# Layer 0: fifteen gathers of slot rows issued one at a time, each after the landing of the one before

## The chip, the cores and the metric

The kernel runs on one core of a Trainium2 chip, written instruction by instruction for five engines (TensorE, VectorE, ScalarE, GpSimd, SyncE) that meet only at semaphores. The metric is the device time of one execution in microseconds, median of several timed executions. A separate execution, taken by the hardware profiler, gives the page and the trace.

## What is computed

Two layers, each a conditioning step and a mixture of experts, on 1024 tokens (32 x 32) of width 256. Layer 0 is where the change is:

```
x1 = x + ffn0(cond0(x)),   x2 = x1 + ffn1(cond1(x1))

cond0:  out[b] = x[b] @ w[subject[b]]                      # one of 8 matrices of 32 x 32 for each b
ffn0:   gate = softmax(xf @ Wr.T)                          # 8 experts
        top-2 experts of each token; rank of the token in its expert; kept if rank <= 320
        y[n] = sum over kept e of gate[n, e] * ((silu(xf @ Wg[e].T) * (xf @ Wu[e].T)) @ Wd[e].T)
```

The capacity of an expert is 320 tokens; an expert's inner width is 176. Layer 1 (a gated unit of width 1024 with adapters, then 16 experts with top 4 and a shared expert) starts from x1, all of it.

## The kernel before

Layer 0 computes two of the eight experts densely for all tokens, and six only for the tokens that chose them. For the six, token rows are brought into slots: 320 slots for each expert, two experts share 640 slots, which are five tiles of 128 (PAIR_TILES); the middle tile of a pair (SHARED_AT = 2) holds 64 slots of each expert. So there are fifteen slot tiles, i = 0 to 14, numbered along the three pairs of experts. The experts are q = 0 to 5.

The stage runs like this:

- All 1024 rows of the conditioned input lie in DRAM (`x2`, written by SyncE). VectorE computes `get`, the token of each slot (L1109, semaphore `q_get`), and `put`, the row of the scatter.
- GpSimd gathers: `gather0(i)` (L603 to L607) issues one indirect DMA of 128 rows of 1 KB, into one of twelve buffers `q_xg`. It counts on `q_in[q]`, 16 for each gather; q is the first expert that needs the tile, so tiles 0, 1, 2 count for expert 0, tiles 3, 4 for expert 1, and so on for each pair. The order of the calls is written out by hand (L615 to L629): five gathers at once, then each further one behind a wait for TensorE (on `q_turn`, an expert's rows transposed, or on `q_gu`, three for each expert, its gate and up products), because it reuses a buffer or to spread the traffic.
- TensorE, for each expert in order: `q_turn_in(q)` waits for `q_in[q]` and transposes the rows (L1573); ScalarE and VectorE split them in two parts (L789 to L793, L1135 to L1139); `q_gate_up(q)` forms the products (L1500 to L1502); ScalarE takes the silu and VectorE the product; `q_down(q)` (L1605, L1606) projects back, with the next expert's transposes and gate products between. ScalarE copies the result out (`q_rows`, L807), VectorE the shared tile (L1156).
- GpSimd scatters: `scatter0` (L609 to L611, shown in the profile as L610) writes each of the fifteen tiles to its rows of `y_k` in DRAM. All scatters stand behind all gathers in GpSimd's program (L632 to L639).
- SyncE waits for all fifteen scatters (L531, L532), loads the rows back (L534), GpSimd, ScalarE and VectorE weigh and add the two choices of each token (L648, L811, L1198), TensorE adds them (L1620) to what the dense experts gave, and VectorE forms x1 (L1205).

The weights of each sparse expert are loaded by SyncE (L503, L510), each waiting for a buffer. TensorE fills the time behind the last sparse expert with products of the dense experts.

Of the kernel before, what the change touches and what calls it, by code (L numbers as in the profile page):

```python
# [31 lines left out]
PAIR_TILES = PAIR_SLOTS // P  # L32
SHARED_AT = CAP // P
# [84 lines left out]
def build(nc, d):  # L118
    with ExitStack() as ctx:
# [264 lines left out]
        q_in, q_st, q_rw, q_dw = t_in[0:ES], s_y[0:ES // 2], s_w1[0:2], s_w1[2:5]  # L384
# [200 lines left out]
        def _(pool):  # L585
# [14 lines left out]
                                  ).then_inc(s_ct, 1)  # L600
            nc.gpsimd.tensor_copy(planes[:].rearrange("p k t -> p (k t)"), cst1[:, CT_TOK:CT_TOK + NT * K1]).then_inc(s_ct, 1)

            def gather0(i):  # L603
                j = i % Q_XG
                q = i // PAIR_TILES * 2 + (i % PAIR_TILES > SHARED_AT)
                nc.gpsimd.indirect_dma_start(q_xg[j], None, d["x2"], bass.IndirectOffsetOnAxis(ap=get[:, i:i + 1], axis=0)
                                             ).then_inc(q_in[q], 16)  # L607

# [6 lines left out]
            for i in range(PAIR_TILES):  # L615
                gather0(i)
            pool.wait_ge(q_turn, 1)
            gather0(PAIR_TILES)
            for n in range(3):
                pool.wait_ge(q_gu, n + 1)  # L620
                gather0(PAIR_TILES + 1 + n)
# [83 lines left out]
        def _(act):  # L705
# [124 lines left out]
            for q in range(ES):  # L830
# [9 lines left out]
                if 2 <= q < 4:  # L840
                    hid_high(L0, q - 2, q - 2)
            _, hi, _ = w_of(ED)
            act.wait_ge(s_raw[0], 32)
            act.wait_ge(q_gu, 3 * (ES - 1))
# [650 lines left out]
        def _(pe):  # L1495
# [356 lines left out]
            def tile_gate_up(i, e):  # L1852
                par, ps = i % 2, tile_gu(i)
                pe.wait_ge(t_xh, i + 1)
                if i == 1:
                    pe.wait_ge(s_silu, 2 * (c + NA))
                elif i == 2:
                    pe.wait_ge(s_prod, 2 * (c + NA))
                elif i > 2:
                    pe.wait_ge(t_hd, i - 1)  # L1860
                whole = [[w[:, bass.ds(e * GU_N, GU_N)] for w in pair_of] for pair_of in ((w1_hi, w1_lo), (w1_hi1, w1_lo1))]
                k_part = [slice(k * P, (k + 1) * P) for k in range(KH)]
                for k, (w_hi, w_lo) in enumerate(whole):
                    T.matmul(ps, xgT_hi[par][:, k_part[k]], w_hi, start=k == 0, stop=False)  # L1864
                    T.matmul(ps, xgT_hi[par][:, k_part[k]], w_lo, start=False, stop=False)  # L1865
                pe.wait_ge(t_xl, i + 1)
                for k, (w_hi, _) in enumerate(whole):
                    last = T.matmul(ps, xgT_lo[par][:, k_part[k]], w_hi, start=False, stop=k == KH - 1)  # L1868
                last.then_inc(t_gu, 1)
# [205 lines left out]
```

## Time and profile before

| | us |
|---|---|
| timed runs, median of 3 | 393.48 |
| lowest and highest | 391.77, 394.31 |
| span of the profiled execution | 424.4 |
| TensorE busy in it | 382.7 |
| GpSimd busy in it | 188.6 |
| mean granted TensorE clock (1.0 is 2.4 GHz) | 0.968 |

The profiled execution is one of its own, 31 us longer than the median of the timed ones; its times are read against its own span. An instruction at GpSimd that issues a DMA is shown for the time of its issue; when the data lands is seen in the chain of waits, or where the DMA engines go idle. The label of a tile is the name of the buffer underneath it: the gathered rows appear as w_hi_f, expert weights as w_hi_f or w_raw, the rows of the scatter as w_dn or sg_b, and the conditioned input as x.

### The profile page before, as it was taken

What the parts mean: (1) busy time and instruction counts of PE and PEld (TensorE: products, weight loads), DVE (VectorE), ACT (ScalarE), POOL (GpSimd) and SP (SyncE); (2) the same over time, 40 slices, a digit from 0 to 9 for tenths busy, and PEclk for the clock granted to TensorE, in tenths of its full rate; (3) what the DMA queues carried; (4) which work ended last, traced back from release to release, by engine and by line L of the source; (5) the groups of instructions that cost most, each with busy time, mean ns of one, the idle gap of its engine ahead of it and who ended that gap; (6) DMA issues with size and microseconds to landing.
All of it is one profiled execution on the core that took longest, in us unless ns stands there. A gap on an engine that the chain in (4) does not pass through costs nothing.

```text
span 424.4 us, 6202 instructions
## 1 busy us (share of the span) xinstructions
PE 382.7 (90%) x1984; PEld 328.6 (77%) x1984; DVE 221.2 (52%) x533; ACT 147.6 (35%) x304; POOL 188.6 (44%) x176
## 2 busy tenths in 40 slices
PE   3998869999999999999999996788987779999996
PEld 3877869787888888888777885687876668899885
DVE  6894554289512211221779763734454324656557
ACT  2644265244534433342554252412122111322140
POOL 0625653563255454423212277355665566444600
PEclk9999989999999999999989999898988898999999
DMA  6965353275233333111013785222222233111285
GB/s 213 386 253 165 101 175 113 74 260 192 88 114 124 125 124 124 39 38 37 2 37 101 181 195 169 62 73 70 85 88 74 72 90 85 61 57 64 77 317 190
DMA packets 22004, 51.89 MB, mean 122 GB/s; under 512 B 3878, under 2 KB 9510, under 8 KB 21670
## 3 DMA queue, kind: packets, MB, share of 16 engines
q1 hardware_dynamic: 16022, 35.24, 25.0%
q0 software_dynamic: 5952, 16.26, 12.6%
q8 instruction: 18, 0.29, 0.3%
q14 instruction: 12, 0.10, 0.1%
HBM read 38.12 MB, written 13.37 MB: 121 GB/s over the span
## 4 chain that ended last, share of the span: by engine, by line
PE 63%; DVE 11%; another core or an unknown queue 9%; DMA 5%; issue 5%; POOL 3%; ACT 2%; SPq 1%; POOLq 0%; DVEq 0%; ACTq 0%
PE gu L1500 9%; PE gu L1501 9%; PE gu L1502 9%; PE y L1889 7%; PE gu L1864 4%; PE gu L1868 3%; PE gu L1865 3%; PE y L1500 2%; PE y L1501 2%; PE y L1502 2%; PE gu L1526 2%; DMA w_raw<-y_k 1%; PE gu L1813 1%; PE gu L1791 1%
## 5 line engine op out<-in xcount | busy, mean ns | idle before, releaser
L591 POOL TENSOR_TENSOR w_lo<-w_raw,w_hi 128x768 fp32r<-128x768 f32 (+3 forms) x26 | 34.4, 1344 | 76.8 <-ACT w_hi L716 60.4
L681 POOL DMA_INDIRECT y_k<-w_raw,put x47 | 46.2, 984 | 49.9 <-DVE w_raw L1417 41.5
L1500 PE MATMUL gu<-act_hi,w_hi 128*128 128x512 f32 x132 | 53.6, 406 | 0.8 <-DVE hid L1023 0.8
L1501 PE MATMUL gu<-act_lo,w_hi 128*128 128x512 f32 x132 | 52.4, 397 | 0.0
L1864 PE MATMUL gu<-w_hi,xgT 128*128 x94 | 40.3, 429 | 12.1 <-ACT xgT L899 8.7
L1023 DVE TENSOR_TENSOR hid<-silu,gu 128x512 f32<-128x512 f32 x24 | 16.5, 687 | 66.6 <-PE gu L1502 66.5
L1502 PE MATMUL gu<-act_hi,w_lo 128*128 128x512 f32 x124 | 48.9, 394 | 0.0
L944 ACT ACTIVATE silu<-gu 128x176 f32<-128x176 f32 x47 | 14.9, 317 | 90.7 <-PE gu L1868 55.8
L1410 DVE TENSOR_TENSOR hid<-silu,gu 128x176 f32<-128x176 f32 x47 | 15.7, 334 | 48.8 <-ACT silu L944 30.6
L1865 PE MATMUL gu<-w_lo,xgT 128*128 x94 | 32.2, 343 | 0.0
L745 ACT ACTIVATE hid_hi<-hid 128x512 fp32r<-128x512 f32 x24 | 15.2, 631 | 47.3 <-DVE hid L1023 47.3
L1864 PEld LDWEIGHTS gu<-w_hi,xgT 128*128 128x128 f32 x94 | 18.9, 201 | 15.5 <-issue 14.3
L1500 PEld LDWEIGHTS gu<-act_hi,w_hi 128*128 128x128 f32 x132 | 25.1, 190 | 6.3 <-DVE hid L1023 1.2
L1501 PEld LDWEIGHTS gu<-act_lo,w_hi 128*128 128x128 f32 x132 | 25.2, 191 | 5.2
L1500 PE MATMUL gu<-lora_store,w_hi 128*128 128x512 f32 (+2 forms) x68 | 25.2, 370 | 4.5 <-DVE lora_store L1135 4.1
L732 ACT ACTIVATE silu<-gu 128x512 f32<-128x512 f32 x30 | 17.7, 595 | 29.8 <-PE gu L1502 29.0
L1502 PEld LDWEIGHTS gu<-act_hi,w_lo 128*128 128x128 f32 x124 | 23.7, 191 | 5.3
L1889 PE MATMUL y<-w_dn,t_hidT 88*128 x96 | 26.6, 404 | 0.0
L1417 DVE COPY w_raw<-y 128x256 f32<-128x256 f32 x47 | 19.7, 418 | 10.5 <-remote 5.2
L1868 PE MATMUL gu<-w_hi,xgT 128*128 x94 | 24.5, 344 | 0.0
L1501 PE MATMUL gu<-lora_store,w_hi 128*128 128x512 f32 (+2 forms) x68 | 24.3, 357 | 0.0
L1889 PE MATMUL y<-w_dn,silu 88*128 x92 | 23.8, 380 | 0.0
(325 smaller groups left out, 905.3 us busy)
## 6 DMA issues: line engine op xcount, KB each, us to landing
w_raw<-in_w_gu SPq DMA_DIRECT2D x16, 352.0 KB, 4.6
w_raw<-in_wc SPq DMA_DIRECT2D x8, 576.0 KB, 5.0
w_raw<-y_k SPq DMA_DIRECT2D x5, 512.0 KB, 5.7
w_hi_f<-in_w0s SPq DMA_DIRECT2D x6, 368.0 KB
y_k<-hid SPq DMA_DIRECT2D x1, 2048.0 KB, 13.3
w_dn<-in_w_dn SPq DMA_DIRECT2D x1, 1936.0 KB
w_raw<-in_ws SPq DMA_DIRECT2D x5, 384.0 KB, 3.0
w_hi_f<-y_k SPq DMA_DIRECT2D x6, 256.0 KB, 4.4
```

The lines of the kernel that those rows point to most:

```text
L591: nc.gpsimd.tensor_tensor(w_lo[par][:, w], w_raw[par][:, w], w_hi[par][:, w].bitcast(F32), ALU.subtract).then_inc(split, 1)
L681: nc.gpsimd.indirect_dma_start(d["y_k"], bass.IndirectOffsetOnAxis(ap=put[:, i:i + 1], axis=0), t_out[j], None).then_inc(s_y[j], 16)
L732: A.activation(silu[s][rows(tail)], gate, ACT.Silu).then_inc(s_silu, 1)
L1023: V.tensor_tensor(out[rows(tail)], silu[s][rows(tail)], up[rows(tail)], ALU.mult).then_inc(s_prod, 1)
L1417: V.tensor_copy(t_out[j], out_ps[i % 2]).then_inc(t_put, 1)
L1500: T.matmul(out, w[0], x[0], start=start, stop=False)
L1501: T.matmul(out, w[0], x[1], start=False, stop=False)
L1502: return T.matmul(out, w[1], x[0], start=False, stop=stop)
L1864: T.matmul(ps, xgT_hi[par][:, k_part[k]], w_hi, start=k == 0, stop=False)
L1865: T.matmul(ps, xgT_hi[par][:, k_part[k]], w_lo, start=False, stop=False)
L1868: last = T.matmul(ps, xgT_lo[par][:, k_part[k]], w_hi, start=False, stop=k == KH - 1)
L1889: last = T.matmul(out_ps[i % 2], t_hidT[i % DEPTH][:, k], w1_dn[0:HALF_I, bass.ds((e * 2 + k) * H, H)], start=k == 0, stop=k == 1)
```

## The change

Ahead of each gather but the first, GpSimd waits until the gather before it has landed: for the count of `q_in` that the previous tile belongs to, at 16 for every gather of that count so far. The function that gives a tile its count gets a name, `pair_of`. The waits for TensorE between the gathers stay, as do their order, buffers and sizes. Scatters and layer 1 are as before.

```diff
+            def pair_of(i):
+                return i // PAIR_TILES * 2 + (i % PAIR_TILES > SHARED_AT)
+
             def gather0(i):
                 j = i % Q_XG
-                q = i // PAIR_TILES * 2 + (i % PAIR_TILES > SHARED_AT)
+                q = pair_of(i)
+                if i:
+                    pool.wait_ge(q_in[pair_of(i - 1)], 16 * sum(pair_of(n) == pair_of(i - 1) for n in range(i)))
                 nc.gpsimd.indirect_dma_start(q_xg[j], None, d["x2"], bass.IndirectOffsetOnAxis(ap=get[:, i:i + 1], axis=0)
                                              ).then_inc(q_in[q], 16)
```

## Rows read from the trace of the kernel before

**Rows 1.** The page: its head and the busy time of each engine.

```profile
span 424.4 us, 6202 instructions
...
PE 382.7 (90%) x1984; PEld 328.6 (77%) x1984; DVE 221.2 (52%) x533; ACT 147.6 (35%) x304; POOL 188.6 (44%) x176
```

**Rows 2.** Timeline, GpSimd: start, duration (us), line, op, out<-in [idle before, releaser].

```profile
29.04 1.14 POOL L606 DMA_INDIRECT w_hi_f<-x,get  x1 [10.04 <-DVE get L1109]
...
37.16 0.94 POOL L606 DMA_INDIRECT w_hi_f<-x,get  x1 [1.93 <-PE y L1573]
...
50.84 0.95 POOL L606 DMA_INDIRECT w_hi_f<-x,get  x1 [0.30 <-issue]
...
54.73 1.00 POOL L610 DMA_INDIRECT y_k<-w_dn,put  x1 [2.95 <-ACT w_dn L807]
...
68.04 0.97 POOL L610 DMA_INDIRECT y_k<-w_dn,put  x1 [4.12 <-ACT w_dn L807]
...
84.10 0.97 POOL L610 DMA_INDIRECT y_k<-w_dn,put  x1 [0.30 <-issue]
```

**Rows 3.** Chain of waits, 28 to 60 us: start, duration (us), what.

```profile
31.75 3.65 DMA w_hi_f<-x,get
...
36.01 0.87 PE y L1573 x6
...
48.55 4.75 another core or an unknown queue
```

**Rows 4.** Timeline, TensorE (L1573 is transposes, L1500 and L1606 products).

```profile
39.08 0.38 PE L1500 MATMUL gu<-lora_store,w_hi 128*128 128x320 f32 x1 [0.41 <-issue]
...
41.79 0.60 PE L1573 MATMUL y<-cst,w_hi_f 128*128 128x128 f32 x4
...
46.57 0.81 PE L1573 MATMUL y<-cst,w_hi_f 128*128 128x128 f32 x6
...
49.38 0.59 PE L1606 MATMUL y<-w_hi_f,w_dn 128*128 128x256 f32 x2
...
59.47 0.38 PE L1500 MATMUL gu<-lora_store,w_hi 128*128 128x320 f32 x1 [2.58 <-DVE lora_store L1135]
...
63.73 0.82 PE L1573 MATMUL y<-cst,w_hi_f 128*128 128x128 f32 x6
...
69.61 0.60 PE L1573 MATMUL y<-cst,w_hi_f 128*128 128x128 f32 x4
...
95.30 1.39 PE L1620 MATMUL y<-cst,w_hi_f 128*128 128x128 f32 x11
```

**Rows 5.** Chain of waits, 80 to 100 us.

```profile
84.10 2.42 DMA y_k<-w_dn,put
...
86.53 0.03 SPq L532
...
98.52 0.68 DVE xT L1205
```

**Rows 6.** Windows: length, busy per engine, TensorE's clock, DMA share, GB/s.

```profile
34.00:36.00 2.00, 0.84 (x8) 0.65 (x6) 1.05 (x2) 1.18 (x2) 0.95 (x1) 1.00 0.99 303
...
39.50:40.50 1.00, 1.00 (x9) 1.00 (x8) 0.00 (x0) 0.27 (x1) 0.04 (x1) 1.00 0.00 0
...
57.00:59.40 2.40, 0.00 (x0) 0.00 (x0) 2.34 (x6) 2.35 (x4) 0.38 (x1) 1.00 0.60 148
...
60.00:62.00 2.00, 2.00 (x9) 2.00 (x9) 1.13 (x2) 0.44 (x1) 1.70 (x2) 0.50 0.27 105
...
86.25:86.50 0.25, 0.25 (x2) 0.20 (x2) 0.22 (x1) 0.25 (x1) 0.25 (x1) 1.00 0.00 0
```

**Rows 7.** Timelines of ScalarE and SyncE, as in rows 2.

```profile
53.32 0.60 ACT L807 ACTIVATE w_dn<-y 128x512 f32<-128x512 f32 x1 [4.77 <-remote]
...
53.31 0.33 SPq L510 DMA_DIRECT2D w_hi_f<-in_w0s  x1
...
81.66 0.60 ACT L807 ACTIVATE w_dn<-y 128x512 f32<-128x512 f32 x1 [2.19 <-PE y L1606]
```

## Prediction

> **What bounds the kernel now.** I read the page's head first: TensorE is busy for 382.7 of 424.4 us, so the kernel as a whole hangs on TensorE and on what it waits for [rows 1]. The change touches one stage, from 29 to 98 us of the profiled execution, so the answer lies in three chains of that stage: the gathers, TensorE, and the scatters behind the gathers.
>
> The timeline of GpSimd shows fifteen gathers at L606, first and last start 29.04 and 50.84 us. An issue takes 0.95 us (the first 1.14) and the next starts 0.30 us later, so a back-to-back gather costs GpSimd 1.25 us; at 37.16 us it waited for TensorE instead [rows 2]. Then come fifteen scatters at L610, from 54.73 to 85.07 us, 0.97 us each plus 0.30 us. They are not back to back: the one at 68.04 us waited 4.12 us for ScalarE's copy L807. So GpSimd has slack in this stage, between 52 and 68 us above all.
>
> TensorE waits for a landing only once: the chain of waits has the third gather as a transfer from 31.75 us for 3.65 us, and after an issue gap the first transposes at 36.01 us [rows 3]. The later groups of transposes (start 41.79, 46.57, 63.73 and 69.61 us for experts 1, 2, 4 and 5; expert 3's are like them) come straight behind a product of TensorE, with no idle time before them [rows 4]. The end of the stage is double. The last scatter is issued at 84.10 us and landed 2.42 us later; only then does SyncE (L532) load the scattered rows back, and the chain of waits runs through this reload to the layer-1 input at 98.52 us [rows 5]. TensorE's own products of the stage last until 95.30 us, where it begins to add the reloaded rows, again without idle time before it [rows 4]. So either chain, if it is later, delays everything after it; the later of the two decides. Layer 1 begins with that input, so what is lost here is lost at the end.
>
> **What one gather costs when the next waits for it.** No row shows this wait, so I bound it. The gather at 37.16 us runs alone: the DMA engines are idle from 39.50 us on [rows 2, 6]. Its data has moved 2.34 us after its issue began. The completion comes after the last packet: of the last scatter, packets end by 86.25 us and the wait ends at 86.52 us, 0.3 us later [rows 5, 6]. So a lone gather lands in 2.34 + 0.3 = 2.64 us. GpSimd's reaction to a semaphore is read at 37.16 us: the transposes it waited for end at 36.88 us, so 0.28 us [rows 2, 3]. Period: 2.9 us in place of 1.25. Lower bound: the scatter's 2.42 us, the same kind of transfer, + 0.28 = 2.7 us [rows 5]. Upper bound: the third gather, beside three weight loads and its two forerunners, took 36.01 - 31.75 = 4.26 us, so 4.5 us with the reaction [rows 3]. I take 2.9, since the DMA engines are free between gathers once those loads are in (share 0.00 from 39.5 to 40.5 us [rows 6]), and 4.26 us for the second gather alone, which is issued at 32.2 us beside those weight loads (DMA share 0.99 from 34 to 36 us [rows 6]). The weight loads that follow later (one pair for each expert, the first at 53.31 us [rows 7]) will meet a gather three or four times; I add 1.5 us for all, and 0 and 6 us are the ends of that.
>
> The Trainium skill has a price of its own (page "DMA: Bandwidth & Descriptors", section on the anatomy of one DMA from GpSimd): about 2.0 us fixed plus the bytes over 436 GB/s, for 128 KB 2.3 us. With the reaction that would be a period of 2.6 us, and by the sums below no loss at all. The row, 2.64 us for the landing, does not agree with it, and I go by the row.
>
> **Step by step.** Gather 0 at 29.04 us. Gather 1 at 29.04 + 0.19 + 2.64 + 0.28 = 32.2 us, landed at 36.4. Gather 2 at 36.7, landed 39.4: the first transposes start at 39.4 instead of 36.0 us. Gathers 3 and 4 land at 42.3 and 45.2; TensorE comes to their transposes 5.8 us after the first ones (41.79 - 36.01 [rows 3, 4]), at 45.2: no further wait. Gathers 5 to 7 are issued at 45.5, 48.4, 51.3 and land by 53.9: expert 2's transposes start at 53.9 instead of 46.6, +7.3 us. Gathers 8, 9 land at 59.7, when TensorE comes to expert 3. Before, the products of expert 3 started only at 59.47 us, after a wait of 2.58 us for VectorE [rows 4]: a chain of ScalarE and VectorE work leads to them that starts with the copy at 53.32 us [rows 7] and takes 6.15 us. It needs expert 0's down products, which ended 3.4 us after expert 2's transposes began (49.97 - 46.57 [rows 4]), so it starts at 57.3 and the products at 63.5 us; at either clock (2.7 or 4.3 us, below) they are over by 67.8 us. Gathers 10 to 12 land at 68.4 against 63.73 (+4.7), 13 and 14 at 74.2 against 69.61 (+4.6). With the 1.5 us of contention the last is issued at 73.1 us and lands at 75.7 (+6.1). GpSimd's older waits for TensorE (on transposes and gate products) are passed long before at each of these times, so they add nothing. From expert 5's transposes to ScalarE's last copy it was 81.66 + 0.60 - 69.61 = 12.65 us [rows 4, 7]: 88.3 us.
>
> **What is queued behind the waiting gathers** is every scatter: none can be issued before gather 14 has been (73.1 + 0.95 us). Scatter 1 then starts at 74.35 instead of 54.73 us, and fifteen at 1.27 us run back to back until 74.35 + 14 x 1.27 + 0.97 = 93.1 us. Are they ready? The last three need the copy at 88.3 us and their turn comes at 89.6 us: yes. Before, the last ended at 85.07 us. So GpSimd's chain is **+8.0 us**, TensorE's only +6.1 us, and the former decides. Behind the scatters, in GpSimd's queue, stand two splits (L642, 3 us, hidden by the reload) and the weighting L648; SyncE's reload of the rows, then its loads of layer-1 weights, wait for the same landing and move with it. I price these at the same +8.0 us, not more, for they keep their order.
>
> TensorE's clock: it idled from 57.0 to 59.4 us and ran at half its speed (granted 0.50, the 1.2 GHz level) at 60 to 62 us; the products from 59.47 to 63.73 us took 4.3 us, those from 39.08 to 41.79 us 2.7 us [rows 4, 6]. After the change TensorE waits 4 us twice (35 to 39, 50 to 54 us) and 2 us before expert 4. Each may cost 1.6 us on TensorE; the first two are covered by the next landing, the third by the 1.3 us between 88.3 and 89.6 us but for 0.3 us. I put 0; without cover it is 1.6 us each.
>
> **The hold.** ScalarE's copy at 53.32 us and SyncE's load at 53.31 us both waited for a product that TensorE had finished by 50.0 us; the chain books 4.75 us on an unknown party [rows 3, 4, 7]. That held up ScalarE, then VectorE, and led to the 2.58 us wait and the half clock. The profiled span of 424.4 us is 31 us above the 393.48 us median of the timed runs, so something in it is not in them. If this hold isn't, the stage before is shorter by the 3.3 us from 50.0 to 53.3 and by the 1.6 us of the half clock (4.3 - 2.7), which comes from the idle time that it leads to: 4.9 us. After the change the gathers set the pace and nothing is gained: the loss would be 8.0 + 4.9 = 12.9 us. I take half of it, 2.4 us. Sum: 393.5 + 8.0 + 2.4 = **403.9 us** (in terms of the profile 424.4 + 8.0 = 432.4 us).
>
> **Rivals.**
> (a) Not slower: a landing costs the 2.42 us of the scatter and nothing contends. Period 2.7, gather 14 at 66.8 us, first scatter at 68.1, last ended at 68.1 + 18.8 = 86.8 us: +1.7 us, 395.2 us. The point from which it decides is a period of 2.57 us, where 29.04 + 14 p + 1.25 + 18.8 is 85.07 us: below it GpSimd's slack between 52 and 68 us swallows everything. By the Trainium skill's price above the kernel would be there, at 393.5 us. Against it: the lone gather's 2.34 us before any completion. If the hold is only in the profile, the point is 2.22 us. Chance 0.11.
> (b) All gathers are as slow as the third was: period 4.5, last scatter 29.04 + 63 + 1.25 + 18.8 = 112.1 us: +27 us, 420.5 us. For it: the gathers share the engines with weight loads. Against: from 39.5 to 40.5 us the engines are idle [rows 6], and the next weight load is issued at 53.31 us [rows 7]. Chance 0.03; a milder form, three or four gathers at 4.3 us (+6 in place of +1.5 us) gives 408.4 us, chance 0.15.
> (c) Faster, since gathers in flight at once were in one another's way: the third took 4.26 us. Its landing would have to come before 36.0 us with two forerunners awaited, and it is issued only at 36.7 us. I see no mechanism; chance 0.02.
> (d) The change does nothing, the waits being met already: excluded for most, as back-to-back issues are 1.25 us apart and a landing takes over 2.4 us; this is included in (a).
> (e) My sum, with the hold in the timed runs (401.5 us) or not (406.4 us): chance 0.69.
>
> **How the numbers follow.** (e) alone spans 400 to 407. The range takes the milder (b) and reaches towards (a): 397.5 to 410 us leaves out most of (a), the strong (b) and (c). About 1%, 3.9 us, is what a measurement of this kernel can tell from no change. Slower by over 1% (above 397.4 us): (b) and (e), 0.87. Within 1%: (a), 0.11. Faster: (c), 0.02.
>
> **What would show it.** In the profile after: starts at L606 about 2.9 us apart (2.6 or less: (a); over 3.5: (b)); first transposes at about 39.4 us; expert 2's at 54 us with a wait of some 4 us on a landing; the last gather at about 73 us; fifteen scatters 1.27 us apart with hardly a wait on L807 between; the last ending near 93 us. I am wrong if the scatters still wait for ScalarE, or if TensorE's products after expert 5 end later than the scatters.

## The result

| | kernel before | changed kernel |
|---|---|---|
| timed, median (us) | 391.77 | 414.8 |
| lowest and highest | 391.32 to 394.31 | 412.5 to 415.5 |
| ratio, 95% interval | | 1.0555 (1.0515 to 1.0595) |
| span of the profiled execution | 424.4 | 410.7 |

The change costs 23.0 us by the medians and 5.6% by the ratio, which is 21.8 us. The forecast had the direction and the order of events right and less than half of the size (10.4 of 23.0 us): 403.9 us, with 410 as the upper end. Medians and ratios here and below leave out executions that lie over 1.5% above the fastest of the same kernel timed beside them, among them one of 475 us and two of 949 us.

The two spans contradict the times: the changed kernel's is the shorter one. The experiments below show that the kernel before takes 425 to 429 us on one chip and 392 to 395 us on three others. The trace that the prediction was made from is like the trace from the first (span 424.4 beside 426.8 us, the same hold), so it is taken to come from a chip of that kind; which chip it was isn't on record. So the readings below set the trace of after beside a second trace of the kernel before, from a chip of the quick kind (run e8_before_again, 392.14 us). Its page, head and busy times:

```profile
span 390.1 us, 6202 instructions
...
PE 369.3 (95%) x1984; PEld 319.4 (82%) x1984; DVE 220.5 (57%) x533; ACT 147.2 (38%) x304; POOL 189.3 (49%) x176
```

and that of the changed kernel, with TensorE's busy share and its granted clock in 40 slices:

```profile
span 410.7 us, 6211 instructions
...
PE 372.6 (91%) x1984; PEld 321.6 (78%) x1984; DVE 221.3 (54%) x533; ACT 147.3 (36%) x304; POOL 190.2 (46%) x176
...
PE   3994848499989999999999999998999999999995
...
PEclk9999989699999999999999999999999999999999
```

Of the 20.6 us by which the span is longer, TensorE is busy for 3.3 us more (372.6 against 369.3 us) and waits for the other 17.3 us. The dents of TensorE's line lie in slices 4 to 8 (31 to 82 us), and the mean clock falls in the same stretch (to 8 and 6 tenths in slices 6 and 8). The rest of the line is nearly as before.

The timeline of GpSimd in the kernel before (e8_before_again), first and last gather, first and last scatter; columns as in [rows 2]:

```profile
29.24 1.14 POOL L606 DMA_INDIRECT w_hi_f<-x,get  x1 [10.27 <-DVE get L1109]
...
50.87 0.95 POOL L606 DMA_INDIRECT w_hi_f<-x,get  x1 [0.30 <-ACT w_dn L807]
52.12 1.00 POOL L610 DMA_INDIRECT y_k<-w_dn,put  x1 [0.30 <-issue]
...
79.30 0.97 POOL L610 DMA_INDIRECT y_k<-w_dn,put  x1 [0.30 <-issue]
```

and in the changed kernel, where L611 is the gather and L615 the scatter:

```profile
29.09 1.14 POOL L611 DMA_INDIRECT w_hi_f<-x,get  x1 [10.07 <-DVE get L1114]
32.24 1.35 POOL L611 DMA_INDIRECT w_hi_f<-x,get  x1 [2.02 <-DMA w_hi_f<-x,get]
37.46 0.94 POOL L611 DMA_INDIRECT w_hi_f<-x,get  x1 [3.87 <-DMA w_hi_f<-x,get]
...
47.31 0.94 POOL L611 DMA_INDIRECT w_hi_f<-x,get  x1 [2.79 <-DMA w_hi_f<-x,get]
...
81.21 0.94 POOL L611 DMA_INDIRECT w_hi_f<-x,get  x1 [2.02 <-DMA w_hi_f<-x,get]
82.46 1.00 POOL L615 DMA_INDIRECT y_k<-w_dn,put  x1 [0.30 <-issue]
...
98.03 0.97 POOL L615 DMA_INDIRECT y_k<-w_dn,put  x1 [0.30 <-issue]
...
100.59 0.97 POOL L615 DMA_INDIRECT y_k<-w_dn,put  x1 [0.30 <-issue]
```

The last gather is issued 30.3 us later (81.21 against 50.87), the last scatter 21.3 us later (100.59 against 79.30). Nine us are taken up by slack that GpSimd had: its last scatter was issued 28.4 us behind the last gather, and back to back it takes 19.4 us (100.59 - 81.21). After the change the scatters do run back to back, as forecast: fourteen steps in 18.1 us, 1.27 us each but for two longer ones.

The chain of waits of the changed kernel (start, duration in us, what) is the landings one after another:

```profile
32.24 4.96 DMA w_hi_f<-x,get
37.20 0.26 issue
37.46 2.85 DMA w_hi_f<-x,get
...
46.60 0.02 POOLq L610
46.61 0.70 issue
...
61.54 4.21 DMA w_hi_f<-x,get
...
100.59 2.41 DMA y_k<-w_dn,put
...
115.05 0.69 DVE xT L1210
```

A "DMA" piece runs from the issue to the landing, the "issue" piece behind it is GpSimd's reaction. The second gather took 4.96 us, one beside a later weight load 4.21 us, one of those at no load 2.85 us. The reaction is 0.26 us at the first four waits. At the nine gathers from 46.61 us on that have an older wait as well it is **0.70 us**: there the wait for the landing (L610) is an instruction of its own, 0.02 us long, and the gather starts 0.70 us after it. The fifteenth gather again has one wait only. The layer-1 input x1 (L1210) begins at 115.05 us; in the trace of e8_before_again it is 93.51 us (a row further down), so 21.5 us of the loss are there by then, against 20.6 us at the end of the span: layer 1 adds nothing.

TensorE, changed kernel: the transposes of experts 0, 2, 4 and 5 (L1578; [rows 4] has them for before):

```profile
40.36 1.54 PE L1578 MATMUL y<-cst,w_hi_f 128*128 128x128 f32 x6 [5.49 <-DMA w_hi_f<-x,get]
...
57.39 1.54 PE L1578 MATMUL y<-cst,w_hi_f 128*128 128x128 f32 x6 [5.64 <-DMA w_hi_f<-x,get]
...
77.55 1.54 PE L1578 MATMUL y<-cst,w_hi_f 128*128 128x128 f32 x6 [5.88 <-DMA w_hi_f<-x,get]
...
85.24 0.66 PE L1578 MATMUL y<-cst,w_hi_f 128*128 128x128 f32 x4
```

It now waits 5.5, 5.6 and 5.9 us for landings where it waited 1.2 us once (and 1.0 us ahead of expert 3's, at 65.79 us), and the transposes take 1.54 us for six where they took 0.81 to 0.87 (36.01 and 46.57 us before).

### The profile page after: what moved, and what is told of

Read it like the earlier page. It is cut to its first block, busy times and chain, and to the rows that moved or that the text cites. A ratio compares the mean times of both kernels' runs of the same rounds, so it can differ in the third digit from the quotient of the medians.

```text
span 410.7 us, 6211 instructions
## 1 busy us (share of the span) xinstructions
PE 372.6 (91%) x1984; PEld 321.6 (78%) x1984; DVE 221.3 (54%) x533; ACT 147.3 (36%) x304; POOL 190.2 (46%) x176
## 4 chain that ended last, share of the span: by engine, by line
PE 63%; DMA 15%; DVE 8%; issue 6%; POOL 5%; SPq 2%; ACT 1%; POOLq 0%; DVEq 0%
DMA w_hi_f<-x,get 9%; PE y L1894 9%; PE gu L1505 8%; PE gu L1507 8%; PE gu L1506 8%; PE gu L1869 4%; PE gu L1873 4%; PE gu L1870 4%; POOL y_k L615 3%; DMA w_raw<-y_k 3%; PE y L1505 2%; PE y L1506 2%; PE y L1507 2%; PE gu L1531 2%; PE y L1521 2%
## 5 line engine op out<-in xcount | busy, mean ns | idle before, releaser
L1869 PE MATMUL gu<-w_hi,xgT 128*128 x94 | 38.6, 411 | 0.7 <-ACT xgT L904 0.7
L611 POOL DMA_INDIRECT w_hi_f<-x,get x15 | 14.8, 986 | 48.3 <-DMA w_hi_f<-x,get 35.7
L1870 PE MATMUL gu<-w_lo,xgT 128*128 x94 | 30.2, 322 | 0.0
L1505 PE MATMUL gu<-lora_store,w_hi 128*128 128x512 f32 (+2 forms) x68 | 24.8, 364 | 1.5 <-DVE lora_store L1140 1.5
L1894 PE MATMUL y<-w_dn,t_hidT 88*128 x96 | 24.5, 379 | 0.0
L1422 DVE COPY w_raw<-y 128x256 f32<-128x256 f32 x47 | 19.8, 421 | 8.4 <-DMA y_k<-w_raw,put 6.7
L1506 PE MATMUL gu<-lora_store,w_hi 128*128 128x512 f32 (+2 forms) x68 | 23.7, 348 | 0.0
L1046 DVE TENSOR_TENSOR hid_lo<-hid,hid_hi 128x512 fp32r<-128x512 f32 x24 | 16.6, 691 | 13.0 <-ACT hid_hi L750 12.9
```

Of the source, the lines that this page charges most:

```text
L1046: V.tensor_tensor(lo[rows(tail)], src[rows(tail)], hi[rows(tail)].bitcast(F32), ALU.subtract).then_inc(s_hl, 1)
L1422: V.tensor_copy(t_out[j], out_ps[i % 2]).then_inc(t_put, 1)
L1505: T.matmul(out, w[0], x[0], start=start, stop=False)
L1506: T.matmul(out, w[0], x[1], start=False, stop=False)
L1894: last = T.matmul(out_ps[i % 2], t_hidT[i % DEPTH][:, k], w1_dn[0:HALF_I, bass.ds((e * 2 + k) * H, H)], start=k == 0, stop=k == 1)
```

## The experiments

Times taken on different occasions are compared by their ratio or difference to the kernel before, timed beside them on the same chip. Each occasion on record was on another chip, so what is said below of a slower chip may as well belong to the occasion.

**The kernel before again.** Unchanged, twice.

> The kernel before, unchanged, profiled once more. The trace of before had a span 31 us above its timed median and a hold of 3.3 us between expert 0's down products and ScalarE's copy; the trace of after has neither (span 410.7 us beside 414.8 us timed). Theory A (the hold and what follows from it belong to that one profiled execution, not to the timed ones): span about 390 us, copy L807 at about 50 us, last scatter issued by about 79 to 80 us, x1 begun near 93.5 us; the stage of after then ends 21 to 22 us later. Theory B (the hold is part of every execution): span near 390 us all the same, but the copy at 53 us and the last scatter ended at 85 us, and the loss of 23 us must come from after x1 for the 6.5 us beyond the 16.5 us seen in the two traces.

Measured: 428.88 us, span 426.8 us, with the timed runs of the kernel before beside it at 424.7 us. The copy L807 of expert 0 comes at 53.09 us and the last scatter is issued at 83.86 us. Neither theory fits as written: by their length the timed executions of this chip have the hold too, but the chip is not the one of the 392 us.

> The kernel before, unchanged, for a trace beside those of this call. If the chip is one where it takes about 392 us: theory A says that the copy L807 of expert 0 comes at about 50 us, with no wait on an unknown party, and x1 begins at about 93.5 us; theory B says the copy at 53 us and x1 at 98.5 us, as in the two traces so far.

Measured: 392.14 us, beside a median of 394.64 us. Theory A. Timeline of ScalarE, the copy; of TensorE, the products of expert 3; and from the chain of waits x1 (L1205):

```profile
50.06 0.60 ACT L807 ACTIVATE w_dn<-y 128x512 f32<-128x512 f32 x1 [1.66 <-PE y L1606]
```
```profile
56.22 0.38 PE L1500 MATMUL gu<-lora_store,w_hi 128*128 128x320 f32 x1 [0.52 <-DVE lora_store L1135]
```
```profile
79.30 2.42 DMA y_k<-w_dn,put
...
93.51 0.69 DVE xT L1205
```

The copy follows TensorE's down products, with no unknown party. The products of expert 3 wait 0.52 us instead of 2.58 and start 3.25 us earlier than in [rows 4], TensorE keeps its full clock, and the last scatter is issued at 79.30 instead of 84.10 us. The hold of [rows 7] and its half clock cost 4.8 us, and this trace of a quick chip has neither. What caused it on the other is open. It is also the smaller part of the difference: the two spans lie 34.3 us apart, of which 5.0 us are there at x1 (98.52 against 93.51 us) and 29.3 us come behind it. The page of the first trace puts 9% of its chain of waits on the unknown party, nearly all of it between 262 and 361 us, in layer 1; the page of e8_before_again has none.

**The changed kernel again.**

> The changed kernel itself, beside the kernel before on one chip (two profiles of the kernel before, with spans of 424.4 and 426.8 us, come from executions 30 us above those timed first; the trace of after does not). Theory A (the loss is the chain of landings plus the scatters behind it, minus a hold of 3.3 us and its half clock where the kernel before has that hold): 23 us where the kernel before takes about 392 us, 16 to 17 us where it takes about 427 us. Theory B (the loss has nothing to do with the hold): 23 us on either.

Measured: 415.66 us against 394.64 us, ratio 1.058 (1.048 to 1.068): the result repeats, 21 to 23 us. No run of the changed kernel itself was made where the kernel before takes 425 us, so theory A's second half is open. Two kernels that end near it were (e2_one_wait, e4_scatters_between). They take 441.0 and 443.0 us beside 424.7 us: 16 and 18 us there, against 16.7 and 23.5 us on quick chips. That would fit a smaller loss beside the hold for the second, but the ratio of the second has an interval of 13 to 24 us, too coarse to show it.

**One wait per gather.** Nine of the fourteen waiting gathers have an older wait for TensorE beside the new one. The experiment drops these, but for one that guards a buffer:

```diff
-            for i in range(PAIR_TILES):
-                gather0(i)
-            pool.wait_ge(q_turn, 1)
-            gather0(PAIR_TILES)
-            for n in range(3):
-                pool.wait_ge(q_gu, n + 1)
...
+            for i in range(Q_TILES):
+                if i == Q_XG:
+                    pool.wait_ge(q_turn, 1)
+                gather0(i)
```

> The changed kernel without the older waits for TensorE between the gathers (one stays, ahead of the thirteenth, whose buffer is used again); each gather still waits for the landing of the one before. In the trace of after the gap from a landing to the next issue is 0.26 us where the gather has that one wait, and 0.70 us at the nine gathers that have an older wait as well. Theory A (the second wait costs 0.44 us at each, though it was met long before): eight of nine go, 3.5 us less, 411.3 us, starts at L611 3.0 to 3.3 us apart. Theory B (the longer gap comes from something else in that stretch, such as traffic): no change, 414.8 us, gaps of 0.70 us as before.

Measured: 441.0 us against 424.7 us, on the slower chip, so it says nothing of the changed kernel's time. The trace decides on the gap. Its chain of waits, sixth and seventh gather, and thirteenth, which keeps both waits:

```profile
49.34 0.26 issue
49.60 2.77 DMA w_hi_f<-x,get
52.38 0.26 issue
...
72.75 0.70 issue
73.44 3.12 DMA w_hi_f<-x,get
```

0.26 us behind the sixth gather, where the changed kernel has 0.70 us, and 0.70 us at the only one with two waits. So the second wait costs 0.44 us, although it had been met some 29 us before. In all these gathers the landing's wait stands behind the older one in the program; what it would cost with the two exchanged was not tried. On a quick chip:

> The changed kernel with one wait per gather, once more, since the first run of it has no timed run of the changed kernel beside it. Its trace already shows gaps of 0.26 us where the changed kernel has 0.70 us. Theory A (the gathers set the pace to the end, so what they save is saved): 3.2 to 3.5 us below the changed kernel, about 17 to 20 us over the kernel before. Theory B (TensorE's chain or the scatters' waits for ScalarE take it back): 21 to 23 us over the kernel before.

Measured: 410.56 us against 393.87 us, ratio 1.042 (1.038 to 1.047): +16.7 us in place of +21 to +23 us. Theory A by the times, which even give somewhat more than the 3.5 us forecast (4.3 to 6.3 us, between runs on different chips). The traces show less: the last gather is issued at 78.87 us (changed kernel: 81.21), and x1 begins at 112.40 us (115.05), 2.3 and 2.7 us earlier. Three landings took longer here (3.77, 3.35 and 3.40 us at the fifth, seventh and eleventh gather, in place of 2.99, 2.69 and 2.8), without a known cause. From the thirteenth landing on the chain of waits no longer runs through the gathers but through TensorE, at half its clock:

```profile
77.27 0.85 PE y L1599 x2
```

So the gathers alone no longer set the pace to the end.

**Two gathers in flight.** The form in which each gather waits for the one two before it wasn't tried: two gathers in flight count on one semaphore, and a wait can't tell which of them has landed.

> The changed kernel, but each gather waits for the landing of the gather two before it, so two may be in flight. Theory A (the loss is latency: one landing of about 2.8 us and a reaction for each gather): two gathers for each such period, 1.8 to 2 us each, the last gather issued near 57 us, where TensorE and not the gathers sets the pace; 392 to 396 us. Theory B (any wait for a landing, with its extra instruction and reaction, is what costs): over half of the 23 us stays, 404 us or more.

In its place, pairs: two gathers back to back, and the next two when both have landed.

```diff
-                if i:
-                    pool.wait_ge(q_in[pair_of(i - 1)], ...)
+                if i and i % 2 == 0:
+                    for last in (i - 2, i - 1):
+                        pool.wait_ge(q_in[pair_of(last)], 16 * sum(pair_of(n) == pair_of(last) for n in range(i)))
```

> The changed kernel, but gathers are issued in pairs: two back to back, and the next two once both have landed. Theory A (the loss is one landing and a reaction for each round of waiting): a round takes 1.25 + 2.9 + 0.3 to 0.7 = 4.5 to 4.9 us for two gathers, 7 rounds, the last gather issued at 29 + 7 x 4.7 = 62 us and, where only the last two groups of transposes wait, 2 to 6 us over the kernel before. Theory B (the cost is in the extra wait instructions and reactions, and not in the landings that nothing hides): half of the loss stays, 8 to 12 us over the kernel before.

Measured: 400.16 us against 394.64 us, ratio 1.018 (1.008 to 1.028), +5.5 us by the medians and +7 by the ratio: at the upper end of theory A's 2 to 6 us and below theory B's 8 to 12, but the interval of the ratio (3 to 11 us) reaches into both. The trace sides with A: its last scatter is issued at 85.24 us, 5.9 us later than in e8_before_again. Half as many rounds of waiting leave a quarter to a third of the loss. The timeline of GpSimd, third, fourth and fifth gather and the last, and the first scatter behind it:

```profile
34.11 0.95 POOL L612 DMA_INDIRECT w_hi_f<-x,get  x1 [2.53 <-DMA w_hi_f<-x,get]
35.36 0.94 POOL L612 DMA_INDIRECT w_hi_f<-x,get  x1 [0.30 <-issue]
38.82 0.94 POOL L612 DMA_INDIRECT w_hi_f<-x,get  x1 [2.51 <-DMA w_hi_f<-x,get]
...
65.17 0.94 POOL L612 DMA_INDIRECT w_hi_f<-x,get  x1 [2.47 <-DMA w_hi_f<-x,get]
66.42 1.00 POOL L616 DMA_INDIRECT y_k<-w_dn,put  x1 [0.30 <-issue]
```

A round is 4.7 us for two (34.11 to 38.82), and 5.1 us on the average of all seven. The last gather is issued at 65.2 us, and the fifteen scatters then still fit until 86.2 us, 6 us late.

**Waits in one part only.** First gathers 1 to 4 (`if 0 < i < PAIR_TILES`), then 6 to 14 (`if i > PAIR_TILES`).

> The waits are kept for gathers 1 to 4 only; the later ten are issued as in the kernel before. In the trace of after the first transposes begin 4.4 us later (40.36 against 36.01) and the second 5.0 us later (46.80 against 41.79), TensorE waiting on a landing for 5.5 us. Theory A (TensorE has no slack this early, so this is lost once and the rest of the loss belongs to the later gathers): 5 us over the kernel before without the hold, 2 to 5 with it. Theory B (the slack of the stage takes it up, since GpSimd's scatters have slack of 4 us at a time): under 2 us.

Measured: 397.76 us against 394.64 us, ratio 1.012 (1.004 to 1.019); the spans of the profiled executions are 395.4 and 390.1 us. Theory A, by the trace: the interval of the ratio starts at 1.7 us, which theory B would allow, but x1 is 6.5 us late. In its trace the first transposes begin at 40.52 us after 5.48 us of idle TensorE, x1 at 100.06 us.

> The waits are kept for the seventh to the fifteenth gather (i > 5) only; the first six are issued as in the kernel before. Theory A (GpSimd's slack between the gathers and its last scatter, 5 us in the clean trace of before, is taken up once; what is over delays the end): the last gather issued at about 70 us instead of 50.9, the last scatter ended at about 90 us instead of 80.3, 10 us over the kernel before; with the 6.5 us that the first five alone cost, less than the 21 to 23 us of the whole. Theory B (parts add up): 15 to 16 us over the kernel before.

Measured: 404.15 us against 393.87 us, ratio 1.027 (1.021 to 1.033): +10.3 us, theory A. The timeline of GpSimd, first gather and last, first scatter and last:

```profile
30.80 1.14 POOL L611 DMA_INDIRECT w_hi_f<-x,get  x1 [11.85 <-DVE get L1114]
...
72.62 0.94 POOL L611 DMA_INDIRECT w_hi_f<-x,get  x1 [2.00 <-DMA w_hi_f<-x,get]
73.87 1.00 POOL L615 DMA_INDIRECT y_k<-w_dn,put  x1 [0.30 <-issue]
...
92.22 0.97 POOL L615 DMA_INDIRECT y_k<-w_dn,put  x1 [0.31 <-issue]
```

From first gather to last scatter's issue it is 61.4 us, before 50.1 us. The two parts give 3 to 5 and 10 us, the whole 21 to 23. In the traces, from first gather to last scatter's issue, it is 6.3 and 11.4 against 21.4 us. Some 1 us of the difference belongs to the wait ahead of the sixth gather, which neither part has. The rest is slack that is counted in both: with the first part alone GpSimd is 9.2 us late at the fifth gather and only 6.3 us at the last scatter, and with the second 20.2 us late at the last gather and 11.4 us at the last scatter, while in the whole only 9.1 us of 30.5 are paid.

**Scatters between the gathers.** Five of the fifteen scatters are issued while the eleventh and twelfth gather are under way:

```diff
             for n in range(3):
                 pool.wait_ge(q_gu, n + 4)
                 gather0(2 * PAIR_TILES + n)
+                if n == 0:
+                    pool.wait_ge(s_cleared, 16)
+                    pool.wait_ge(q_put, 1)
+                if n < 2:
+                    scatters(n)
...
+            for q in range(2, ES):
+                scatters(q)
```

> The changed kernel with expert 0's two scatters issued behind the eleventh gather and expert 1's three behind the twelfth, in the time of the landings; ten scatters are left behind the last gather. Theory A, that of the prediction (the queue of fifteen scatters behind the gathers decides the end of the stage): five scatters less at the end, 6.4 us less 1 us by which the last gathers are late, 409.5 us. Theory B (TensorE's own chain from the last landing is as late: in the trace of after the last copy L812 starts at 97.36 us and the first scatter that needs it at 98.03 us): no gain, 414 to 416 us.

Measured: 443.02 us against 424.7 us, ratio 1.044 (1.031 to 1.057), on the slower chip, an interval (13 to 24 us) that decides nothing; on a quick one:

> The changed kernel with five of the fifteen scatters issued between the gathers, once more: its first run was where the kernel before takes 428 us, with no timed run of the changed kernel beside it. Theory A (the queue of scatters behind the gathers decides the end): 5 us below the changed kernel, 16 to 18 us over the kernel before. Theory B (TensorE's chain from the last landing is as late, so the scatters wait for ScalarE's last copies instead): 21 to 24 us over the kernel before, and waits of 2 to 3 us on the copy between the last scatters.

Measured: 416.09 us against 392.64 us, ratio 1.059 (1.053 to 1.064), +23.5 us. Theory B: no gain at all from ten scatters instead of fifteen at the end. The timeline of GpSimd has the reason, last gather and three of the scatters behind it:

```profile
82.44 0.94 POOL L611 DMA_INDIRECT w_hi_f<-x,get  x1 [2.08 <-DMA w_hi_f<-x,get]
85.94 1.00 POOL L615 DMA_INDIRECT y_k<-w_dn,put  x1 [2.56 <-ACT w_dn L818]
...
96.83 0.97 POOL L615 DMA_INDIRECT y_k<-w_dn,put  x1 [2.98 <-ACT w_dn L818]
...
102.00 0.97 POOL L615 DMA_INDIRECT y_k<-w_dn,put  x1 [0.30 <-issue]
```

The scatters wait 2.56 and 2.98 us for ScalarE's copies, and the last is issued at 102.00 us with ten behind the gathers, at 100.59 us with fifteen. The last gather itself is 1.2 us later than in the changed kernel, since the scatters ahead of it take GpSimd's time. TensorE's chain from the last landings is as late as the queue of scatters was, and half clock makes it later: behind its third wait (6.95 us) TensorE runs at a granted clock of 0.50 until 84 us, and expert 5's transposes begin at 87.51 us, although gather 14 landed at 85.8 us.

**The weight loads moved.** SyncE's loads at 31.9 to 32.8 us wait until the first three gathers have landed.

```diff
                 if q >= 2:
                     sp.wait_ge(q_wlo, q - 1)
+                if q == 2:
+                    sp.wait_ge(q_in[0], 16 * (SHARED_AT + 1))
```

> The changed kernel, with the three weight loads that SyncE issues at 31.9 to 32.8 us held until the first three gathers have landed. In the trace of after the second gather, beside these loads, took 4.96 us to land, the others mostly 2.7 to 3.1 us. Theory A (traffic of the weight loads makes a landing slow): the second gather lands in 2.7 to 3 us and the first transposes begin 2 us earlier; the slow landing moves to the fourth or fifth gather, and the time stays within 1 us of the changed kernel's. Theory B (the second landing is slow for another reason, such as its longer issue of 1.35 us): it stays near 5 us.

Measured: 413.64 us against 393.87 us, ratio 1.052 (1.047 to 1.057). Theory A in its order of events. Its chain of waits, second, third and fourth gather:

```profile
33.04 3.12 DMA w_hi_f<-x,get
...
36.42 2.83 DMA w_hi_f<-x,get
...
39.51 3.80 DMA w_hi_f<-x,get
```

The second gather lands in 3.12 us instead of 4.96, and the fourth, now beside the loads, in 3.80 instead of 2.75. Over half of the gain is lost again there. From first to last gather it is 50.3 us, in the changed kernel 52.1 us; the time is +19.8 us, 1 to 3 us below the changed kernel's +21 to +23, more than the 1 us of theory A.

The same edit in the kernel before:

> The kernel before with the same edit of SyncE and nothing else. TensorE waits 1.0 us for the third gather there (36.05 us), which shares the DMA engines with these loads. Theory A (the loads delay that gather, and nothing needs the loaded weights before 43 us): first transposes at about 35.0 us, 1 us less at the end, 0.3%, at the edge of what can be measured. Theory B (the loads come late instead, or fourth and fifth gathers do): no change, or slower by up to 2 us.

Measured: 392.02 us against 393.87 us (12 and 16 runs), ratio 0.9967 (0.9939 to 0.9994). Theory A: from first gather to x1 it is 63.3 us, in e8_before_again 64.3 us, and TensorE's transposes start without a wait:

```profile
35.48 0.87 PE L1575 MATMUL y<-cst,w_hi_f 128*128 128x128 f32 x6
```

It is the fastest of these kernels, by 0.3%, with an interval that just excludes no change.

## Why the prediction was wrong

The mechanism held and its terms were too small. Of the 12.6 us between the forecast and the measured difference, 8.1 us are the period of the gathers and 2.4 us the half of the hold; the other 2.1 us are within what the medians move.

**Right.** The mechanism and its order. Landings one after another pace GpSimd; scatters, queued behind, run back to back at 1.27 us; the last ones end the stage; layer 1 neither adds nor gives back. The first transposes came at 40.4 us (forecast 39.4), the wait for expert 2's was 5.6 us (4). The rival of no loss, and with it the price in the Trainium skill (page "DMA: Bandwidth & Descriptors", section on the anatomy of one DMA from GpSimd; an estimate of 2.3 us for 128 KB by its fit), was rightly held unlikely: no landing of the chain was under 2.69 us.

**Wrong, first: the period.** I put the last gather's issue at 73.1 us; it was 81.21 us, 8.1 us later. Two terms of the sum were too small.
- The reaction. I read 0.28 us at a gather that waits for TensorE and took it for all fourteen, 3.9 us. But the change puts a second wait ahead of nine gathers that had one, and those take 0.70 us. In all 5 x 0.26 + 9 x 0.70 = 7.6 us, so 3.7 us were missing. The prediction even said that the older waits "add nothing", since they would be met long before. That is the step of the reasoning that failed: an added wait was priced only by what it waits for, and the cost of having a wait more was shown at 0.44 us by e2_one_wait. [rows 2] could not show it, for no gather there has two waits.
- The landing. 14 landings took 44.2 us (81.21 - 29.09 - 7.6, with 0.3 us of gaps), forecast 40.3. The second took 4.96 instead of 4.26 us. The undisturbed ones took 2.7 to 2.85 instead of 2.64 us, and the two that met a weight load in mid-stage (issued by SyncE at 62.2 and 69.1 us) 4.21 and 3.58 us; with some of about 3.1 us for which I have no cause, that is 3.9 us more than forecast, the 1.5 us for traffic included. e11_loads_later shows for the first three loads that they do this; for the later ones it is only that the times agree. The last 0.5 us are gaps of 0.02 us and rounding.

**Wrong, second: the hold.** I halved it, at 2.4 of 4.9 us. On a chip that is as quick as the timed runs (e8_before_again) the kernel before doesn't have it, and its last scatter ends at 80.27 instead of 85.07 us, 4.8 us earlier: the sum was right, the half was not. My ground was that the profiled span lay 31 us above the median, so that something in the trace was not in the timed runs. That pointed the right way, but I had put the cause in profiling and not in the chip.

**Together.** 8.0 us (GpSimd's chain) + 8.1 (period) + 4.8 (hold) = 20.9 us. The traces of the quick chips have 21.5 us at x1 and 20.6 us in the span, and the ratio of the timed runs gives 21.8 us; the 23.0 us of the medians are 1.5 to 2.4 us above the traces, within what the medians of the kernel before move between occasions (391.8 to 394.6 us).

**Right for the wrong reason: which chain decides.** I put GpSimd's chain 1.9 us behind TensorE's and said that the scatters decide. e4_scatters_between and e13_scatters_between_again say that they don't decide alone: with five scatters moved away nothing is gained. In the trace of after ScalarE's last copy ends at 97.96 us and the first scatter that needs it is issued at 98.03 us. The 1.3 us that I had left between the two (88.3 and 89.6 us) went into one landing: the last gather, issued at 81.21 us, took 4.0 us to land and not 2.64, beside loads that SyncE issued at 82.54 and 82.91 us, so that TensorE came to expert 5's transposes only at 85.24 us. Both chains carry the 8.1 us, so the total isn't touched by it. To shorten the queue of scatters alone does nothing (e13_scatters_between_again); that to shorten TensorE's chain alone would do nothing either follows from scatters that are back to back, and was not tried.

**TensorE's clock.** Its transposes behind each of the three waits of 5.5 to 5.9 us ran at the 1.2 GHz level, and in between it rose again. This was forecast, and put at 0 because the next landing covers it. The trace of the changed kernel agrees: behind the first wait TensorE comes to its next transposes 0.2 us after the landing that they need (46.80 against 46.57 us), behind the second 1.0 us before it, and behind the third both come at 85.2 us. But the cover is thin. In e9_one_wait_again and e13_scatters_between_again it is gone, and TensorE's products at half clock stand in the chain of waits: from expert 4's transposes to the end of ScalarE's last copy they take 21.0 and 21.5 us, in the changed kernel 20.4 and in e8_before_again 18.5 us. Two windows of the changed kernel, columns as in [rows 6]; the lower line is the earlier stretch, behind the first wait, at a granted clock of 0.50; the upper one, at 1.00, has TensorE at work without a wait since 57.39 us:

```profile
62.00:64.00 2.00, 2.00 (x15) 1.97 (x15) 0.00 (x0) 1.77 (x3) 0.49 (x1) 1.00 0.45 53
41.00:43.00 2.00, 2.00 (x12) 2.00 (x11) 0.10 (x1) 0.94 (x3) 0.52 (x1) 0.50 0.22 66
```

## What to carry to other kernels

A wait for a landing cost the landing, a reaction of 0.26 us, and, where the gather had a wait already, 0.44 us more: count the waits of each instruction after the change, also those long met. When the parts of a change are timed alone, their losses can add up to less than the whole, because the same slack pays for each of them. And before the trace is used for a sum, compare its span with the timed median: where they differ by 8%, look for stretches in which an engine waits for nothing that the profile can name, and take them out whole.

## What was not expected of the hardware

- An indirect gather at GpSimd with one wait was issued 0.26 us after the landing that it waited for, one with two waits 0.70 us after it, although the other wait had been met 5 to 29 us before.
- A gather of 128 rows of 1 KB landed 2.69 to 3.14 us after the start of its issue in the changed kernel's trace when no weight load was under way, and 3.6 to 5.0 us beside weight loads of 256 to 384 KB.
- The same kernel took 392 to 395 us on four occasions, on three chips at least, and 425 to 429 us on one, on another chip. In the profile that goes with the slower one, ScalarE and SyncE both noticed a product of TensorE 3.3 us after its end (50.0 and 53.3 us [rows 4, 7]); in that of e8_before_again no such delay stands at this copy.
